# Attention by tiles of 128 queries and 16 heads in one stream of full steps, with the mask added on TensorE

## The reference, cut to what matters

```python
# x: (2, 2048, 1024) fp32; 32 query heads of 32, ONE key/value head of 32; causal
q = (x @ wq_w.T + wq_b).reshape(b, t, 32, 32)
k, v = x @ wk_w.T + wk_b, x @ wv_w.T + wv_b            # (b, t, 32)
scores = einsum('bqhd,bkd->bhqk', q, k) / sqrt(32)      # causal: -inf above the diagonal
attn = einsum('bhqk,bkd->bqhd', softmax(scores), v)
x = layernorm(x + attn.reshape(b, t, 1024) @ wo_w.T + wo_b)
x_scale, w_scale = 448 / max|x|, 448 / max|weight|      # over the whole tensors
y = clip(x * x_scale, -448, 448) @ clip(weight * w_scale, -448, 448) / (x_scale * w_scale)
return layernorm(x + y)
```

## Time and profile before

| | us |
|---|---|
| median of 3 runs (lowest, highest) | 2720.03 (2715.79, 2721.07) |
| the profiled execution, its own time | 2719.72 |
| its span, first to last instruction | 2718.0 |
| granted TensorE clock, mean | 0.974 of full |
| TensorE matmul busy | 2542.1 (94%) |
| VectorE busy | 1879.0 (69%) |
| ScalarE busy | 1273.5 (47%) |
| GpSimd busy | 865.6 (32%) |

### The profile page before, as it was taken

The page is one execution under the profiler, slowest core; times in us unless marked ns, Lnnn a source line. Parts: engine busy times, 40 slices in busy tenths (PEclk is TensorE's granted clock), DMA queues, the critical chain, the costliest instruction groups (busy, mean ns, idle before and its releaser), DMA issues.

```text
span 2718.0 us, 45333 instructions
## 1 busy us (share of the span) xinstructions
PE 2542.1 (94%) x15400; PEld 1588.6 (58%) x15400; DVE 1879.0 (69%) x1432; ACT 1273.5 (47%) x1571; POOL 865.6 (32%) x569
## 2 busy tenths in 40 slices
PE   7999998889999999999878999999999997799998
PEld 5888885545544444444544555444444445688887
DVE  6343336668788889999555788888899993444444
ACT  2222224545566666777334565666777670100000
POOL 2321302433322222212334333222221223566663
PEclk9999998989999999999888999999999998899999
DMA  7343334411211111011233122111101104122221
GB/s 232 124 145 141 116 128 141 122 40 51 62 45 39 39 40 40 12 39 40 67 95 94 44 66 51 40 39 39 40 29 37 39 1 162 48 85 90 88 93 62
DMA packets 75076, 197.24 MB, mean 73 GB/s; under 512 B 8559, under 2 KB 8559, under 8 KB 72815
## 3 DMA queue, kind: packets, MB, share of 16 engines
q1 hardware_dynamic: 50220, 140.52, 17.9%
q10 hardware_dynamic: 24768, 55.59, 5.3%
HBM read 123.72 MB, written 72.35 MB: 72 GB/s over the span
## 4 chain that ended last, share of the span: by engine, by line
PE 62%; issue 7%; DVE 5%; ACT 5%; POOL 3%; DMA 1%; ACTq 1%; SPq 0%; DVEq 0%; POOLq 0%
PE bank L1165 16%; PE bank L1177 15%; PE bank L1153 13%; PE bank L1261 13%; ACT prob L689 4%; DVE acc L940 3%; PE bank L1195 2%; POOL prob L546 2%; PE bank L1187 2%; DMA q_st<-max_d 1%; PE bank L1250 1%; DVE acc L937 1%; POOL att_lo L538 0%; ACT att_hi L700 0%; DVE r_den L901 0%
## 5 line engine op out<-in xcount | busy, mean ns | idle before, releaser
L689 ACT ACTIVATE prob<-bank 128x1024 f32<-128x1024 f32 (+3 forms) x1280 | 1077.4, 897 | 627.6 <-PE bank L1165 595.2
L940 DVE TENSOR_TENSOR acc<-acc,prob 128x2048 f32<-128x2048 f32 (+3 forms) x512 | 1093.4, 2136 | 131.1 <-POOL prob L546 85.8
L1165 PE MATMUL bank<-q_st,keys 98*128 98x512 f32 (+3 forms) x2560 | 712.5, 392 | 88.6 <-ACT prob L689 63.0
L1165 PEld LDWEIGHTS bank<-q_st,keys 98*128 98x128 f32 x2560 | 427.6, 192 | 391.6 <-ACT prob L689 308.3
L1177 PE MATMUL bank<-prob,v_t 128*32 128x512 f32 (+3 forms) x5120 | 596.6, 548 | 11.1 <-POOL prob L546 11.1
L546 POOL TENSOR_SCALAR_AFFINE_SELECT prob<-prob 128x512 f32<-128x512 f32 x256 | 300.8, 1179 | 873.0 <-ACT prob L689 872.4
L1075 PE MATMUL bank<-xt_hi,w_hi 128*128 128x512 f32 x576 | 227.3, 395 | 16.4 <-DVE xt_lo L777 15.7
L1075 PE MATMUL bank<-xt_hi,w_lo 128*128 128x512 f32 x576 | 226.6, 393 | 0.0
L1075 PE MATMUL bank<-xt_lo,w_hi 128*128 128x512 f32 x576 | 226.2, 393 | 0.0
L1177 PEld LDWEIGHTS bank<-prob,v_t 128*32 128x32 f32 x5120 | 107.9, 109 | 197.8 <-issue 141.4
L1261 PE MATMUL bank<-wf_hi,xs_hi 128*128 128x512 f32 x512 | 202.8, 396 | 0.0
(11 more groups left out here) (118 smaller groups left out, 2668.7 us busy)
## 6 DMA issues: line engine op xcount, KB each, us to landing
q_st<-q_hi_d SPq DMA_DIRECT2D x128, 256.0 KB
xt_raw<-x_t SPq DMA_DIRECT2D x16, 1024.0 KB, 6.9
q_hi_d<-part_hi ACTq DMA_DIRECT2D x64, 256.0 KB, 2.1
q_lo_d<-part_lo ACTq DMA_DIRECT2D x64, 256.0 KB, 2.3
q_st<-q_lo_d SPq DMA_DIRECT2D x64, 256.0 KB
x<-x_d SPq DMA_DIRECT2D x32, 512.0 KB, 3.2
out<-y ACTq DMA_DIRECT2D x32, 512.0 KB, 2.6
res<-x SPq DMA_DIRECT2D x24, 512.0 KB, 4.0
```

What stands on the lines that cost most here:

```text
L689: nc.scalar.activation(prob[:, t % SLOTS, 2 * p:2 * p + 2, off:NB], bank[:, 2 * p:2 * p + 2, off:NB], ACT.Exp, scale=SCALE).then_inc(p_don ...
L940: nc.vector.tensor_tensor(acc[:, r, :, off:NB], acc[:, r, :, off:NB], new, ALU.add).then_inc(acc_done, 1)
L1165: last = nc.tensor.matmul(bank[:, h, off:NB], keys[:, b * JB + t // QT, t % QT * P:(t % QT + 1) * P], q_st[:, slot, h, off:NB], start=True ...
```

## The change

Attention is cut the other way: a group is now one tile of 128 queries by 16 heads, so that a row of scores is 4 heads of 128 queries and each step is full, 512 columns by 4. A tile `i` of a batch has `i + 1` key tiles; the diagonal one comes first (`key_tile`). 64 groups have 544 steps in all. Tiles are taken in pairs, a long one with a short one, 34 steps a pair (`PAIR`), both batches in one list; every engine's list is written out in full (no hardware loops) against one count of steps. In step `t == 0` four bf16 matmuls of 512 columns add the mask to the scores (`same_bf`, `later_bf`), and GpSimd's `affine_select` and the semaphore `masked` go. The output bias enters through one more matmul for each half of a tile (`share`, `bo_parts`) instead of an add on GpSimd. All but the last tile are projected inside the stream at places in the list `names`: ScalarE's rounding at `SPLIT`, TensorE's matmuls from `HALF0` to `HALF0_END` and from `HALF1` to `HALF1_END`, VectorE's sums at `SUM0` and `SUM1`, the scaling at `SCALE_ROW`, the largest value at `LARGEST`. The scaling of the layer norm moves from VectorE to ScalarE (an activation with scale and bias), for which GpSimd makes a third value, the shift (`shift_of`). The queries have three buffers and are loaded two groups ahead, in runs of 512 bytes. The clips of the weight come every six steps from the start. In the third stage only the counts of some waits change.

```diff
+            bo_parts = sb("bo_parts", [P, D], F32R, s)
...
+            q_st0 = sb("q_st0", [SM, 2 * HG, 2 * P], F32R, s)
+            q_st1 = sb("q_st1", [SM, 2 * HG, 2 * P], F32R, s)
...
+            q_st = [t[:].rearrange("p h (c n) -> p (h c) n", n=P) for t in (q_st0, q_st1, q_st2)]
...
+            same_bf = sb("same_bf", [P, P], BF16, s)
+            later_bf = sb("later_bf", [P, HG, P], BF16, s)
...
+        PAIR = 2 * (TT + 1)
+        pairs = [(b, k) for b in range(B) for k in range(TT // 2)]
+        tiles = [(b, i) for b, k in pairs for i in (TT - 1 - k, k)]
+        groups = []
+        for p in range(len(pairs)):
+            a, c = 2 * p, 2 * p + 1
+            if p < len(pairs) - 1:
+                groups += [(a, 0), (c, 0), (a, 1), (c, 1)]
+            else:
+                groups += [(a, 0), (a, 1), (c, 0), (c, 1)]
+        lengths = [tiles[q][1] + 1 for q, u in groups]
+        begins = [sum(lengths[:n]) for n in range(len(groups))]
+        steps = [(n, t) for n in range(len(groups)) for t in range(lengths[n])]
+        STEPS = len(steps)
+        SLOTS_OVER = 14
+        den_at = []
+        for n in range(len(groups)):
+            at = begins[n] + lengths[n] + 1
+            den_at.append(max(at, den_at[-1] + 4) if n else at)
...
+        def places(q):
+            p, second = divmod(q, 2)
+            if p < len(pairs) - 2:
+                names = (21, 24, 29, 30, 32, 37, 38, 40, 42) if second else (4, 7, 12, 13, 15, 20, 21, 23, 25)
+                base = (p + 1) * PAIR
+            elif p == len(pairs) - 2:
+                names = (17, 20, 23, 24, 26, 29, 30, 32, 33) if second else (4, 7, 10, 11, 13, 16, 17, 19, 20)
+                base = (p + 1) * PAIR
+            else:
+                names = (39, 40, 40, 41, 40, 40, 41, 42, 43) if second else (30, 33, 34, 35, 36, 37, 38, 39, 40)
+                base = p * PAIR
+            return [base + at for at in names]
...
+        SPLIT, HALF0, HALF0_END, SUM0, HALF1, HALF1_END, SUM1, SCALE_ROW, LARGEST = range(9)
+        split_at, sum0_at, sum1_at = at_place(SPLIT), at_place(SUM0), at_place(SUM1)
+        scale_at, largest_at = at_place(SCALE_ROW), at_place(LARGEST)
+        fillers = {}
+        for q in range(TILES):
+            at = places(q)
+            for half, first, last in ((0, at[HALF0], at[HALF0_END]), (1, at[HALF1], at[HALF1_END])):
+                for place in range(first, last + 1):
+                    fillers.setdefault(place, []).append((q, half, place - first, last - first + 1))
+        PIECE_EVERY, PIECE_CLIP = 6, 4
...
+        def key_tile(s):
+            n, t = steps[s]
+            b, i = tiles[groups[n][0]]
+            return b * TT + (i if t == 0 else t - 1)
...
+            for s in range(STEPS + SLOTS_OVER):
+                if s < STEPS:
+                    n, t = steps[s]
+                    if t == 0 and n >= 1 and n + 2 < len(groups):
+                        sp.wait_ge(s_done, 2 * s + 1)
+                        load_queries(n + 2)
+                        load_maxima(n + 2)
...
+                if s in split_at:
+                    q = split_at[s]
+                    if q >= 2:
+                        sp.wait_ge(x1_sent[q % 2], 16 * (q // 2))
+                        sp.wait_ge(ln1, (q - 1) * LN)
+                    sp.dma_start(res[:, q % 2], x_tiles[tile_row(q)]).then_inc(res_in[q % 2], 16)
+                if s - 1 in scale_at:
+                    q = scale_at[s - 1]
+                    sp.wait_ge(ln1, q * LN + LN - 1)
+                    sp.dma_start(x1_d[tile_row(q)], res[:, q % 2]).then_inc(x1_sent[q % 2], 16)
+            sp.wait_ge(spread_done, len(groups))
+            sp.wait_ge(piece_sent, 16 * KT)
...
+            def shift_of(moments, done, before):
+                wait_apart(pool, done, before + (NH + 3))
+                nc.gpsimd.tensor_scalar(moments[:, 3:4], moments[:, 0:1], moments[:, 2:3], -1.0, ALU.mult, ALU.mult).then_inc(done, 1)
...
-                            wait_apart(pool, p_done, s0 * 2 + (2 * t + 4))
-                            tri = prob[:, t % SLOTS, :, off:off + P]
-                            nc.gpsimd.affine_select(out=tri, in_=tri, compare_op=ALU.is_ge, fill=0.0, base=0,
-                                                    pattern=[[0, HG], [1, P]], channel_multiplier=-1).then_inc(masked, 1)
...
+            pool.wait_ge(wo_cut, KT)
+            nc.gpsimd.memset(share[:].bitcast(F32), 2.0 / P).then_inc(fixed, 1)
+            nc.gpsimd.tensor_copy(same_bf[:], ident[:]).then_inc(fixed, 1)
...
+            nc.gpsimd.affine_select(out=later_bf[:], in_=later_bf[:], compare_op=ALU.is_ge, fill=MASKED, base=0,
+                                    pattern=[[0, HG], [1, P]], channel_multiplier=-1).then_inc(fixed, 1)
+            for s in range(STEPS + SLOTS_OVER):
+                if s in split_at:
+                    q = split_at[s]
+                    pool.wait_ge(att_hi_cut, q + 1)
+                    nc.gpsimd.tensor_tensor(att_lo[:], att[:, q % TILES_KEPT], att_hi[:].bitcast(F32), ALU.subtract).then_inc(att_cut, 1)
+                if s in sum1_at:
+                    q = sum1_at[s]
+                    inverse_deviation(moments[:, q % 2], ln1, q * LN)
+                    shift_of(moments[:, q % 2], ln1, q * LN)
...
+            for s in range(STEPS + SLOTS_OVER):
+                if s < STEPS:
+                    act.wait_ge(pv_done, s + 1)
+                    act.wait_ge(acc_done, s + 1)
+                    for p in range(2):
+                        act.wait_ge(s_done, 2 * s + p + 2)
+                        nc.scalar.activation(prob[:, s % SLOTS, 2 * p:2 * p + 2], bank[:, 2 * p:2 * p + 2], ACT.Exp, scale=SCALE).then_inc(p_done, 1)
+                if s - 2 in group_of_end:
+                    n = group_of_end[s - 2]
+                    q = groups[n][0]
...
+                    act.wait_ge(pv_done, s - 1 + SLOTS)
+                    if q >= TILES_KEPT:
+                        act.wait_ge(att_cut, q - TILES_KEPT + 1)
+                    nc.scalar.activation(attended(n), bank[:, 4 + n % 2], ACT.Copy).then_inc(pv_moved, 1)
+                if s in split_at:
+                    q = split_at[s]
+                    act.wait_ge(att_ready, last_group[q] + 3)
+                    act.wait_ge(y_done, 2 * q)
+                    nc.scalar.activation(att_hi[:], att[:, q % TILES_KEPT], ACT.Copy).then_inc(att_hi_cut, 1)
+                if s in scale_at:
+                    q = scale_at[s]
+                    act.wait_ge(ln1, q * LN + LN - 2)
+                    nc.scalar.activation(res[:, q % 2], res[:, q % 2], ACT.Identity, bias=moments[:, q % 2, 3:4], scale=moments[:, q % 2, 2:3]).then_inc(ln1, 1)
...
+            for s in range(STEPS + SLOTS_OVER):
+                if s < STEPS:
+                    n, t = steps[s]
+                    new = prob[:, s % SLOTS]
+                    if t <= 1:
...
+                    if t == 0 and lengths[n] == 1:
+                        dve.wait_ge(p_done, 2 * s + 4)
+                        nc.vector.tensor_copy(acc[:, n % 2], new).then_inc(acc_done, 1)
+                    elif t == 1:
+                        dve.wait_ge(p_done, 2 * s + 4)
+                        nc.vector.tensor_tensor(acc[:, n % 2], prob[:, (s - 1) % SLOTS], new, ALU.add).then_inc(acc_done, 2)
+                    elif t > 1:
+                        dve.wait_ge(p_done, 2 * s + 4)
+                        dve.wait_ge(acc_done, s + SLOTS)
+                        nc.vector.tensor_tensor(acc[:, n % 2], acc[:, n % 2], new, ALU.add).then_inc(acc_done, 1)
+                if s - 1 in group_of_den:
+                    invert(group_of_den[s - 1])
+                if s - 3 in group_of_den:
+                    normalise_group(group_of_den[s - 3])
...
+                if s in sum0_at:
+                    add_residual(sum0_at[s], 0)
+                if s in sum1_at:
+                    q = sum1_at[s]
+                    add_residual(q, 1)
+                    dve.wait_ge(y_read, 2 * q + 2)
+                    moments_of(res[:, q % 2], stats[:, q % 2], moments[:, q % 2], ln1, q * LN)
+                if s in largest_at:
+                    q = largest_at[s]
+                    dve.wait_ge(ln1, q * LN + LN - 1)
+                    nc.vector.tensor_reduce(amax_x[:, q:q + 1], res[:, q % 2], AX.X, ALU.max, apply_absolute_value=True).then_inc(ln1, 1)
...
+            def scores(s):
+                n, t = steps[s]
+                if t == 0:
+                    pe.wait_ge(q_in[n % 3], 64 * (n // 3 + 1))
+                queries = q_st[n % 3].rearrange("p (a g) n -> p a g n", g=HG)
+                k = key_tile(s)
+                for p in range(2):
+                    pe.wait_ge(p_done, 2 * s + p + 1)
+                    for g in (2 * p, 2 * p + 1):
+                        last = nc.tensor.matmul(bank[:, g].rearrange("p (a n) -> p a n", n=P), keys[:, k // QT, k % QT * P:(k % QT + 1) * P], queries[:, :, g], start=True, stop=(t > 0))
```

(23 more changed lines are left out.)

454 lines of the change are left out of this document (121 added, 333 removed).

## The result

| | before | after |
|---|---|---|
| median, same chip (lowest, highest) | 2718.28 (2715.79, 2721.07) | 2840.13 (2839.81, 2840.46) |
| ratio, 95% interval | | 1.0448 (1.0430, 1.0466) |
| span of the profiled execution | 2718.0 | 2838.2 |
| granted TensorE clock, mean | 0.974 | 0.951 |
| first product of the third stage at | 2332.5 | 2453.4 |

The changed kernel is 4.5% slower; 2795 was forecast, with 2640 to 2850 as the range. The third stage is as long as before, so all of it lies ahead of 2453.4 us, where the forecast had 2408: the sum missed 45 of 121 us.

A forecast was written before the change was run, and what follows sets the result against it. TensorE was taken to set attention's pace, VectorE close behind. 451.3 + 0.5 + stream 1716 + wait 138 + clock 33 + end 69 = 2408 us for the last stage's first product, +75.5; forecast 2795 us, own range 2735 to 2855.

The forecast's parts named there:

- The step that decides: Scaling on ScalarE: VectorE's adds lock out GpSimd's small operations, ScalarE waits, then TensorE, and the clock falls.
- one add blocks, not two: Rival at the scaling: 2.3 us a tile less, 2726 us, or 2693 if the clock then holds; chance 0.11.
- The wait: TensorE waiting for ScalarE at each tile's scaling: 4.6 us x 30 tiles = 138 us.
- 7.4 us: End of VectorE's residual add and moments, counted from the start of the last step with projection matmuls.
- The clock: TensorE's clock falling behind the idle at each tile's scaling: 33 us, bounds nothing and 65 us.
- The rounding of `att_hi`: ScalarE's rounding inside the stream: 30 x 0.84 = 25 us.
- the prices: Attention's full steps: 3.05 us with four projection matmuls, 3.50 with six, 2.12 with none.
- The end: From the stream's end to the last stage's first product: 69 us in all.
- The loads' 6 us: SyncE sends for the last stage's weight only after the last tile is stored: 6 us, between 0 and 12.
- The clip's unexplained idle: GpSimd's first clip starts after 9.48 us idle; if a branch stall that leaves with the loops, some 5 us lower.
- Steps, groups, bias, queries: Stream terms: steps 1491 us, groups 122 us, bias matmuls 14 us, query loads nothing.
- The mask: 256 bf16 matmuls on TensorE at 0.23 us each, with nothing to hide them: 59 us.

The follow-up runs named there:

- e2: Changed kernel with GpSimd's three small layer-norm operations put on VectorE, a reciprocal replacing the power (output not the layer norm): 2677.85 us.
- e1: Changed kernel with the scaling and the largest value of 29 tiles three steps later: 2621.28 us, 0.9636 of the kernel before.
- e11: Changed kernel with 12 to 26 unread matmuls per tile, fitted to fill TensorE's idle ahead of the scores that wait for the scaling: 2789.78 us.
- e7: e1 with seven of the eight loads of the last stage's weight ahead of the last tile's store: 2610.01 us.
- e4: Changed kernel without its 256 mask matmuls, so its output differs: 2794.68 us.
- e8: e1 with the mask back on GpSimd as two affine selects of 1024 elements a group, no mask matmuls: 2570.86 us.
- e10: Changed kernel with the mask alone back on GpSimd, the scaling on ScalarE at its unchanged place: 2796.3 us.
- e3: Changed kernel with 20 unread matmuls of 512 columns ahead of the scores that wait for the scaling, in each of 30 tiles: 2820.84 us.

## Why the prediction was right, and where its sum was off

*The step that decides was right.* Scaling, ScalarE's wait, TensorE's wait and the clock came as written. The lock as the prediction read it in the earlier trace rows holds for the 2048-element adds for their full 2.29 us: the first operation took 2.06 us, against 1.72 beside the shorter add. By the Trainium skill (SBUF — State Buffer, "SBUF: two separate sides") such an operation is locked out for the whole instruction; the trace agrees, and e2, which takes GpSimd out of it, got 162 us back. The rival "one add blocks, not two" is refuted: in each of the 29 tiles in which VectorE was adding two operations were held, and in e1 mostly the third as well.

*The wait was under-sized: 4.6 us a tile against 5.85.* On average the step with the wait took 7.87 us, in e1 2.47, and 0.45 us comes in the next one (3.84 us in e11 against 3.38 in e1): 170 us in 29 tiles (28 with the wait and one that had none; the last one's lies in the end), not 138 in 30. The term that was too small rests on "7.4 us" for the end of the moments. In the tile shown it is 9.2 (1101.44 - 1092.23), and all that follows is late by the same 1.8 us: shift 14.7 instead of 12.9, TensorE 16.9 instead of 15.2. VectorE's list has the group's product with the spread denominators ahead of the residual sum (1098.47), and this waits for TensorE's spreading in the very step. I had counted spreadings as absorbing the wait; here one prolongs it. This is so in 18 tiles. In four of those without that product the moments ended at 7.3 us, as counted, and TensorE began at 14.6. No run takes the product out of the way, so this reading rests on the traces alone. The scaling itself took 1.24 us, not 1.06.

*The clock was under-sized: 33 us against 50* (e11), because all 28 such idles inside the stream brought it down and each cost 1.8 us, not 1.3; 65 was the bound.

*The rounding of `att_hi` was over-sized:* 25 us, where e1's four steps stand 11 us above the prices in all.

Together the steps around the scaling are 230 us above the prices and not 196: 34 us of the missed 45.

*The end:* from the last step's scores to the first product 85 us against 74 by the prediction's terms (2408 less the 2334 at which they put those scores). The loads' 6 us were 11 (e7), inside the bounds of 0 and 12. The other 6 are the last tile's scaling, which the prediction had among its 30 waits: the stream's last values wait 3.25 us for ScalarE, and by estimate TensorE loses 2.7 us more at the lower clock until 2384.

```profile
2378.10 1.94 PE L1158 MATMUL bank<-prob,v_t 128*32 128x512 f32 x8 [3.25 <-ACT prob L697]
```

The clip's unexplained idle stayed though attention's loops have gone from GpSimd's list: the clip of row 2443.62 starts 7.4 us after VectorE's second operation. So the 5 us that were to leave with those loops did not. The Trainium skill (Runtime: NRT & Kernel Launch, "Instruction fetch mechanics") says that a taken branch can stall instruction fetch; no run here shows such a stall, and the cause of this idle stays open.

*Steps, groups, bias, queries:* right within some 3 us in all. Projection steps outside the scaling sum to 1115.5 us where the prices gave 1114.7; TensorE never waited for queries.

*The mask:* 59 us forecast; 44 to 50 came back when it went (e4, e8, e10), since a part lies beside waits. The price was right, the judgement of the exchange was missing: I said that TensorE has nothing to hide these matmuls, but not that full steps hide GpSimd's selects: TensorE waited 0.6 us for them in all of e8.

## What to carry to other kernels

Before an operation moves to an idle engine, ask how near that engine stands to the bottleneck and what its input waits for: ScalarE was busy for 46%, but one late exponential stops TensorE, whereas VectorE at 61% could wait behind four buffers. When an engine's result is late, look first at who locks it out, then move its reader down its list until the result is there: three steps here, which cost nothing. Work that must overlap is best left on the engine with time to spare (GpSimd's mask), even where TensorE needs less than half as long for it (four matmuls of 0.23 us against two selects of 1.09).

## What the runs showed of the hardware that was not expected

- In e3 the granted clock fell behind an idle of 1.65 us, with 4.8 us of matmuls ahead of it, in 15 of 18 tiles and stayed up in three; with 0.29 us left in e11 it fell in none.
- `affine_select` of 128x1024 takes 1.09 us on GpSimd; begun during an add of VectorE it ended 0.95 to 0.97 us behind the add, 3.21 us after its start at worst (e8). It goes the other way too: an add whose start lies 0.02 us behind that of a select (1192.19) took 3.22 us instead of 2.29.
- GpSimd's operations on one element are held by each add in turn: three in a row took 2.06, 2.56 and 1.89 us in a tile of e1 where alone they take 0.22, 0.57 and 0.26.
